# Row numbers of a three-layer decoder from one-hot products, with the order changed at attention's ends and in the second half

## The reference

```python
x = _layernorm(x + _L0_attn_ref(x, ...))     # causal attention, 16 heads of 32
x = _layernorm(x + _L0_xattn_ref(x, itok, ctx, ctx, ctx))
#   expert of a token: min(token id // 6250, 3); y = (silu(x @ W.T) * (x @ W.T)) @ W.T, W = ctx[expert]
x = _layernorm(x + _L0_ffn_ref(x, ...))
#   8 experts of width 352, the top 2 by softmax, weighted by their probabilities,
#   plus sigmoid(x @ Wsg) * shared, a gated product of width 1408
```

## Time and profile before

| | |
|---|---|
| runs, us | 1242.27, 1242.53, 1243.09 (median 1242.53) |
| the profiled execution, us | 1241.76, span 1239.0 |
| busy share of the span | TensorE 95%, VectorE 55%, ScalarE 37%, GpSimd 23% |
| TensorE's clock, mean granted | 0.979 of full |
| granted clock 32 to 36, 36 to 38, 38 to 40, 60 to 74 | 1.00, 0.60, 0.55, 0.50 to 0.57 |
| granted clock 602 to 679, 1057 to 1067, 1083 to 1117 | 1.00, 0.83, 1.00 |
| attention, second layer, third layer | 0 to 434, 435 to 571, 571 to 1239 |
| shared steps 2 to 21, experts' tiles, steps 22 to 43 | 602 to 772, 772 to 1041, 1034 to 1228 |
| loading of a ScalarE function table, us | 1.28, four times |

### The profile page before, as it was taken

How to read it: one execution, slowest core, us unless ns; L and a number is a source line. 1 busy time by engine, 2 the same in 40 slices (tenths; PEclk the granted TensorE clock), 3 DMA queues, 4 the chain that set the end, 5 groups by cost and what they waited for, 6 DMA issues and landing times.

```text
span 1239.0 us, 20363 instructions
## 1 busy us (share of the span) xinstructions
PE 1173.0 (95%) x6452; PEld 934.7 (75%) x6452; DVE 684.7 (55%) x1490; ACT 453.6 (37%) x703; POOL 279.8 (23%) x405
## 2 busy tenths in 40 slices
PE   7789999999998789998999999999999998899996
PEld 5556666676675568887777888899999997778885
DVE  5575666656656647765467434434434433676744
ACT  3245434435436223322333333344444433233331
POOL 3012314414415401223123430000000001442302
PEclk8989999999999989999999999999999999899998
DMA  7347673522533233333165673345345423555530
GB/s 249 79 117 245 197 270 102 138 68 80 144 85 112 93 119 93 114 117 119 35 96 144 235 267 105 124 138 168 132 152 158 160 76 117 167 177 164 169 120 34
DMA packets 128814, 169.76 MB, mean 137 GB/s; under 512 B 18112, under 2 KB 71360, under 8 KB 128704
## 3 DMA queue, kind: packets, MB, share of 16 engines
q1 hardware_dynamic: 110368, 128.77, 34.6%
q0 software_dynamic: 10336, 32.53, 7.3%
q10 hardware_dynamic: 8000, 7.10, 2.4%
HBM read 95.98 MB, written 47.19 MB: 116 GB/s over the span
## 4 chain that ended last, share of the span: by engine, by line
PE 73%; DVE 8%; DMA 7%; POOL 3%; ACT 2%; issue 2%; SPq 2%; ACTq 2%; POOLq 0%; DVEq 0%
PE bank L852 27%; PE bank L915 13%; PE psT L482 12%; PE psS L548 3%; DMA shared_raw<-in_L_ffn_Sd_dram 3%; PE psO L587 3%; PE bank L1547 2%; PE bank L1548 2%; PE bank L1549 2%; PE psE L569 2%; PE psN L587 2%; SPq L362 2%; PE bank L1569 1%; POOL routed_rows_io L1454 1%; DVE shared_held L1871 1%
## 5 line engine op out<-in xcount | busy, mean ns | idle before, releaser
L915 PE MATMUL bank<-store,shared_held 128*128 128x512 f32 (+1 forms) x840 | 188.4, 380 | 7.5 <-DVE shared_held L1871 7.2
L915 PEld LDWEIGHTS bank<-store,shared_held 128*128 128x128 f32 x840 | 152.5, 189 | 39.6 <-DVE shared_held L1871 9.9
L482 PE MATMUL psT<-store 128*128 128x512 f32 x576 | 157.6, 409 | 4.7 <-DVE store L701 3.0
L657 ACT ACTIVATE acc<-psE 128x512 f32<-128x512 f32 x160 | 92.7, 598 | 133.1 <-PE psE L569 88.8
L787 DVE CUSTOM_DVE_ANT_0 psS<-psS,attn_mask 128x512 f32<-128x512 f32 (+3 forms) x256 | 119.8, 512 | 35.3 <-PE psS L548 35.1
L482 PEld LDWEIGHTS psT<-store 128*128 128x128 f32 x576 | 106.2, 195 | 24.4 <-issue 3.4
L1454 POOL DMA_INDIRECT routed_rows_io<-sorted_y,routed_pos x32 | 36.8, 1149 | 380.2 <-DMA sorted_y<-routed_rows_io 313.0
L852 PE MATMUL bank<-shared_held,routed_h_hi 128*128 x624 | 115.8, 328 | 0.3 <-DVE routed_h_lo L1912 0.3
L424 POOL TENSOR_SCALAR_AFFINE_SELECT acc<-acc 128x256 f32<-128x256 f32 (+1 forms) x160 | 56.9, 362 | 258.7 <-ACT acc L657 258.3
L852 PEld LDWEIGHTS bank<-shared_held,routed_h_hi 128*128 128x128 f32 x624 | 100.3, 188 | 1.2 <-issue 0.9
L852 PE MATMUL bank<-store 128*128 x351 | 91.4, 404 | 0.0
(11 more groups left out here) (270 smaller groups left out, 2015.4 us busy)
## 6 DMA issues: line engine op xcount, KB each, us to landing
sorted_x<-attn_zero SPq DMA_DIRECT2D x19, 768.0 KB, 6.2
shared_raw<-in_L_ffn_Sg_dram SPq DMA_DIRECT2D x44, 256.0 KB, 3.1
shared_raw<-in_L_ffn_Su_dram SPq DMA_DIRECT2D x44, 256.0 KB, 3.6
shared_raw<-in_L_ffn_Sd_dram SPq DMA_DIRECT2D x44, 256.0 KB, 4.8
routed_rows_io<-sorted_x SPq DMA_DIRECT2D x39, 256.0 KB, 2.9
sorted_y<-routed_rows_io SPq DMA_DIRECT2D x39, 256.0 KB, 2.1
attn_qS<-attn_ch_hi SPq DMA_DIRECT2D x128, 64.0 KB
routed_gu_raw<-in_L_ffn_Wg_dram SPq DMA_DIRECT2D x8, 704.0 KB, 4.5
```

What stands on the lines that cost most here:

```text
L482: last = pe.matmul(out, lhs[a](k), rhs[c](k), start=(s[-1] == 0 and k == 0), stop=(s[-1] == 2 and k == KC - 1))
L657: act.activation(p_f[:, u, :], psE[:, n % 2, :], ACT.Exp, scale=SCALE).then_inc(exp_done, 1)
L915: last = pe.matmul(out, w[:, slot, at + k * P:at + (k + 1) * P], x_part(k), start=(g == 0 and k == 0), stop=(g == 2 and k == KC - 1))
```

## The change

1. **Row numbers.** `token_rows`, `number`, the sixteen scatters and the read are gone. `place` is kept as float32. After step 10 VectorE works out each token's tile and row within it (`token_tiles`), after steps 12 and 13 a one-hot matrix of the rows (`token_hot`), and ahead of step 15 TensorE adds sixteen bf16 products of 128x128 by 128x32 (`tokens`); VectorE reads them (`read_tokens`) before it goes on with step 15. TensorE's third of the six product groups of `shared_up(15)` waits for that read. SP waits for the numbers in step 16, GpSimd before the first gather.
2. **Second half.** Tile 0 is added after step 23, tiles 1 and 2 after step 24, the others after step 22 + t as before; tiles 0 to 7 are normed one step later. Of the last four tiles, ScalarE scales and shifts three (`centre` on VectorE makes the shift), and VectorE's gated adds stand one tile ahead of the statistics.
3. **Attention's start.** `wp_lo` is made by GpSimd. All twelve K transfers of group 2 are SP's, and ScalarE issues none for it.
4. **Attention's end.** The last sequence's PR, LN1, LN2 and ST follow each other tile by tile. The last four CW tiles come with one transfer after the first PV of the last group, and go through four banks that are free by then, without the shared ones.
5. The semaphores `ident_done`, `onehot_done` and `place_done` are merged with others, with the counts adapted.

```diff
@@ attention_steps
-    steps += product("PR", b, 0) + product("PR", b, 1) + [("LN1", b, 0)]
-    steps += product("PR", b, 2) + [("LN2", b, 0), ("LN1", b, 1), ("ST", b, 0)]
-    steps += product("PR", b, 3) + [("LN1", b, 2), ("LN2", b, 1), ("LN1", b, 3), ("ST", b, 1)]
-    for i in (2, 3):
-        steps += [("LN2", b, i), ("ST", b, i)]
+    steps += product("PR", b, 0) + [("LN1", b, 0)] + product("PR", b, 1) + [("LN1", b, 1), ("LN2", b, 0), ("ST", b, 0)]
+    steps += product("PR", b, 2) + [("LN1", b, 2), ("LN2", b, 1), ("ST", b, 1), ("LN2", b, 2), ("ST", b, 2)]
+    steps += product("PR", b, 3) + [("LN1", b, 3), ("LN2", b, 3), ("ST", b, 3)]
     steps += [("CW", n) for n in range(10, 16)]
@@ attention, SP
-                    for r, part in enumerate(parts[:3 - qk]):
+                    for r, part in enumerate(parts[:2] if qk == 1 and g > 2 else parts):
                         for i in range(4):
-                            if (qk, g, r) == (1, 2, 1):
-                                continue
                             sp.dma_start(dst[r * D:(r + 1) * D, i, :].bitcast(F32),
...
+                if s == ("PV", NG - 1, 0):
+                    sp.wait_ge(pv_done, QT * (NG - 1) + 1)
+                    sp.dma_start(p_f[:, 0:KC, :], ctx_w[E - 1].rearrange("(k p) n -> p k n", p=P)).then_inc(w_in[3], 16)
@@ attention, GpSimd ahead of its steps
+            pool.wait_ge(w_hi_done, 5)
+            pool.tensor_tensor(wp_lo[:], p_f[:, 0:4, :], wp_hi[:].bitcast(F32), ALU.subtract).then_inc(wp_lo_done, 1)
@@ attention, ScalarE
-                    if qk == 1 and g >= 2:
+                    if qk == 1 and g > 2:
...
@@ attention, VectorE
-                    if s == ("V", 0, 2, 2):
-                        dve.wait_ge(w_hi_done, 5)
-                        dve.tensor_tensor(wp_lo[:], p_f[:, 0:4, :], wp_hi[:].bitcast(F32), ALU.subtract).then_inc(w_lo_done, 1)
@@ routed_phase
-        FINAL_AT = {PART + t: t for t in range(HALF * QT)}
+        FINAL_AT = {PART + 1 + t: t for t in range(HALF * QT)}
...
-        ADD_AT = {PART + t: t for t in range(NT)}
+        TOKEN_AT = 15
+        ADD_AT = {PART + 1: [0], PART + 2: [1, 2]}
+        ADD_AT.update({PART + t: [t] for t in range(3, NT)})
@@ routed_phase, GpSimd
-            for t in range(NT):
-                pool.wait_ge(s_h, 1 + t // 2)
-                pool.indirect_dma_start(out=token_rows, out_offset=bass.IndirectOffsetOnAxis(ap=place[:, t:t + 1], axis=0),
-                                        in_=number[:, t:t + 1], in_offset=None).then_inc(ids_out, 16)
...
             def store_out(t):
-                pool.wait_ge(out_done, t + 1)
+                if t in LAST[:-1]:
+                    pool.wait_ge(shifted_out, t - LAST[0] + 1)
+                else:
+                    pool.wait_ge(out_done, min(t, LAST[0]) + 1)
@@ routed_phase, TensorE
+            def tokens():
+                pe.wait_ge(sel_done, 3)
+                pe.wait_ge(s_h, TOKEN_AT - 1)
+                out = s_up[TOKEN_AT % 2][:, 0:2 * NT]
+                for t in range(NT):
+                    last = pe.matmul(out, hot[:, t, :], halves[:, t].rearrange("p h j -> p (h j)"), start=(t == 0), stop=(t == NT - 1))
+                last.then_inc(count_full, 1)
@@ routed_phase, ScalarE, after its last unit
+            for i, t in enumerate(LAST[:-1]):
+                act.wait_ge(centred, i + 1)
+                act.activation(acc[:, t, :], acc[:, t, :], ACT.Identity, bias=minus_mean[:, t:t + 1], scale=rstd[:, t:t + 1]).then_inc(shifted_out, 1)
@@ routed_phase, VectorE
+            def token_tiles():
+                dve.wait_ge(consts, 7)
+                shape = [P, NT, NT]
+                then(dve.memset(upto[:, :, NT], 0.0))
+                then(dve.tensor_tensor(upto[:, :, 0:NT], bcast(place[:], shape, 2), bcast(iota128[:], shape, 1), ALU.is_ge))
+                then(dve.tensor_reduce(tiles_up, upto[:, :, 0:NT], AX, ALU.add))
+                then(dve.scalar_tensor_tensor(inner, tiles_up, -float(P), place[:], ALU.mult, ALU.add))
+                then(dve.tensor_tensor(in_tile, upto[:, :, 0:NT], upto[:, :, 1:NT + 1], ALU.subtract))
+                then(dve.tensor_scalar(halves[:, :, 0, :], in_tile, pcol, None, ALU.mult))
+                then(dve.tensor_tensor(halves[:, :, 1, :], in_tile, bcast(iota128[:], shape, 2), ALU.mult))
+
+            def token_hot(part):
+                tiles = slice(part * NT // 2, (part + 1) * NT // 2)
+                shape = [P, NT // 2, P]
+                dve.tensor_tensor(hot[:, tiles, :], bcast(inner[:, tiles], shape, 2), bcast(irow, shape, 1), ALU.is_equal).then_inc(sel_done, 1)
...
-            for i, t in enumerate(LAST):
-                shared_out(NQ - 1, [i])
+            shared_out(NQ - 1, [0])
+            dve.wait_ge(s_read, LAST[0] + 1)
+            moments(LAST[0])
+            shared_out(NQ - 1, [1])
+            make_h(HALVES + 1)
+            low_h(HALVES + 1)
+            for i, t in enumerate(LAST[1:], 1):
                 dve.wait_ge(s_read, t + 1)
                 moments(t)
-                if i == 0:
-                    make_h(HALVES + 1)
-                    low_h(HALVES + 1)
-                if i:
-                    normalise(t - 1)
+                centre(t - 1)
+                if i + 1 < QT:
+                    shared_out(NQ - 1, [i + 1])
             normalise(LAST[-1])
```

More of the change, by code:

```diff
@@ L146, in attention_phase @@
     for s in steps:
-        if s[0] in SHARED and (s[0] not in PARTS or s[-1] == 0):
+        if s[0] in SHARED and not (s[0] == "CW" and s[1] >= (E - 1) * KC) and (s[0] not in PARTS or s[-1] == 0):
             key = s[:-1] if s[0] in PARTS else s
@@ L762, in _ @@
                     then(dve.tensor_reduce(picked1, picked, AX, ALU.add))
-                    dve.tensor_copy(place[:], picked1).then_inc(place_done, 1)
-                    dve.wait_ge(place_done, 1)
+                    then(dve.tensor_copy(place[:], picked1))
                 elif kind in ("Q", "K") and s[-1] == 2:
@@ L1173, in chosen_phase, with routed_phase @@
     return [(stored[r], 16 * ((NS - r + 3) // 4)) for r in range(4)]
-def routed_phase(nc, sems, store, ident, powm, acc, x2_in, x2_of, packed, place, number, token_rows, weights, bank, chosen_y, chosen_stored, out_dram, sorted_x, sorted_y, experts, shared):
+def routed_phase(nc, sems, store, ident, powm, acc, x2_in, x2_of, packed, place, weights, bank, chosen_y, chosen_stored, out_dram, sorted_x, sorted_y, experts, shared):
     NT, C = acc.shape[1:]
@@ L1469, in _ @@
                     pool.drain()
-                if n in ADD_AT and ADD_AT[n] + 2 < NT:
-                    gather(ADD_AT[n] + 2)
+                for t in ADD_AT.get(n, []):
+                    if t + 2 < NT:
+                        gather(t + 2)
                 if n in FINAL_AT:
@@ L2057, in _ @@
                     shared_out(HALF)
-                if n in ADD_AT:
-                    routed_add(ADD_AT[n])
+                for t in ADD_AT.get(n, []):
+                    routed_add(t)
                 if n in FINAL_AT:
```

119 lines of the change are left out of this document (78 added, 41 removed).

## The result

The changed kernel takes 1227.88 us in the median of four runs (1224.78 to 1229.22), the kernel before 1242.4 beside it (1242.06 to 1243.09): a ratio of 0.9873, 95% interval 0.9851 to 0.9894. The forecast was 1225.5 with a range to 1232. The profiled execution took 1227.31 with a span of 1225.6, 13.4 less than the span before. By execution times it is 14.5 less: the profiled execution before was 2.8 us longer than its span, this one 1.7.

What follows compares the result with a forecast made beforehand. TensorE, 95% busy, bounds the kernel, so only its gaps and slow stretches are worth anything. 3.5 + 2.8 + 2.4 + 3.3 - 1.2 + 4.7 + 1.4 = 16.9 us won gives 1225.5 us, range 1219.5 to 1232 (8 in 10).

Steps and rivals of the forecast that it cites:

- Part 1: Attention's first group: wp_lo on GpSimd removes TensorE's wait (2.0 us) and the slow clock behind it (1.5): 3.5 us won.
- Rival D: Attention's first group: GpSimd's wp_lo split blocks VectorE's row maxima, 2.8 us lost there, 1231.8 us in all; chance 0.05.
- Part 2: Attention's group 2: K stacks all on SP free ScalarE's exponential, TensorE's idle goes: 2.8 us won, bounds 0 to 5.3.
- rival B: Attention's group 2: K stacks on one queue land after 73, gaining 0, 1228.3 us in all; chance 0.12.
- so the gain lasts: Attention's group 1: K reaches ScalarE's queue 3.5 us sooner, and its twelve issues are the path to 54.3.
- Part 3: Attention's end: tile-by-tile order issues the last scatter near 427.7 in place of 430.03: 2.4 us won, bounds 1.0 to 3.0.
- Part 4: Shared steps: dropping four-byte-row scatters wins 3.3 us (2.95 late steps, 0.3 first gathers); sixteen added products cost 1.2 with the switch.
- Part 5: Second half: later adds remove TensorE's 6.9 us stop and slow clock; 4.7 us won by up(32), bounds 3.0 to 8.7.
- VectorE then bounds the steps with adds and a norm: Second half, steps 23 to 30: these steps take 8.57 us against 8.19, giving back some of the gain.
- Rival A: Second half, step 24: two gather pairs stop TensorE near 3 us and the clock falls; 1228.5 us in all; chance 0.12.
- Part 6: Tail: VectorE loses two normalisations and one gated add, gains two tiny products: 1.4 us won, bounds 0.5 to 2.

Runs made afterwards that it cites:

- part 1 undone: Changed kernel with wp_lo split by VectorE after V of the third tile again, as before: 1232.66 us, ratio 0.9918 to the kernel before.
- two zero-writes: Changed kernel with two zero-writes per attention group in place of four: 1227.08 us alone; with GpSimd's fills held back and power ahead of gathers too, 1219.91 us.

## Why the prediction was right, point by point

- **Part 1** was right in size: 3.5 forecast, 3.6 in the trace. Its two terms do not stand alike. The wait, 2.0, came back when the part was undone (2.2 at group 1). The slow clock behind it, 1.5, did not: it followed waits of 1.86 and 1.83 us in the two profiles with the old attention, and not the 1.93 us of the kernel with part 1 undone. So the 3.5 holds against an execution in which the clock fell there, and I had taken that as given; how often it falls, three profiles don't tell. The two things I had left open came out as taken: GpSimd's long split, 4.61 us where I had estimated 5.1, held no row maximum up (0.70 us). Rival D falls. The rule of the Trainium skill, "SBUF — State Buffer", "Who interferes with whom", on the shared port pair agrees: the maxima have one SBUF input. The same rule is what the start shows from the other side: weight splits with two SBUF inputs beside GpSimd's fills took 5.59 us in place of 2.45. I had weighed the rule for the instruction that the change moved, and not for the overlaps that were there already and that the missing iota shifts.
- **Part 2** was mis-sized by 0.6: 3.4 against 2.8. The stacks landed in time (a wait of 0.20 us), and rival B falls. The 2.8 was TensorE's idle time alone; the low clock around it, 60 to 74 in the table before, lasted only from 60 to 67 this time, which the sum had not counted. How much of the 0.6 that is, no run separates.
- **What the sum lacked** is a term between the parts: "so the gain lasts" holds for the gap of group 1 and not, in this pair of profiles, for the groups that follow, in which 2.2 us were given back. Of that 0.7 lie between 113 and 155 us, in the stretch of SyncE's queue. Another 0.8 lie between K of group 15 and the first projection product: the clock granted from 385 to 389 was 0.57 in the changed kernel, with nearly the same waits as before, where it had been full. This is chance: four profiles had it full there and took 57.9 to 58.1 us, ten had it low and took 58.4 to 58.8. Whether the change gives anything back at all is open. From the first scores of group 2 to the first projection product it is 336.2 us in the profile before and 338.4 in the changed kernel, but 338.5 in the kernel before without its four-byte scatters, which has the old attention, and 337.6 to 338.9 in the others with four zero-writes. Only with two zero-writes is it as short as before (335.5 and 336.1).
- **Part 3** failed in size, 1.6 against 2.4. The last add came at 421.12, 11.7 us behind the first projection product where it had been 11.2, as in the new order VectorE ends the third tile's norm first. What I hadn't counted is the third scatter, which stands ahead of the last power on GpSimd: issued at 422.42 for 0.96 us, it held the power 0.5 us beyond its statistics. The forecast 3.2 us from add to scatter were 3.7.
- **Part 4** was right in its gain (2.8 of 2.95 when nothing else was changed; 0.4 for the gathers). The sixteen products cost 0.4 us in place of 1.1: the step ahead of them lasts 8.61 us where the others last 8.19. Their starts stand 0.025 us apart, and the 0.56 of the row holds the length of the last one too. I had taken 0.07 from two neighbours. Whether the scatters slowed the loads by their size or by their number, no run separates.
- **Part 5** was right in its sum, 4.4 in the trace and 4.7 when undone, and wrong in a cause. "VectorE then bounds the steps with adds and a norm" was a wait for GpSimd's power behind two gathers. The profile before had it: in rows 8 GpSimd's second gather is issued at 1105.31 for 0.95 us, the power comes behind it, and only then, at 1107.43, VectorE's split. I took the length of the step and did not ask what filled it. So the number came out right for a reason that was wrong, and would have misled in the next change: VectorE's work was not what had to be cut.
- **Rival A** is real and a matter of chance: in three of seven profiles the clock fell at the 2.85 us stop so that it cost 1.6 us, in the one taken for the changed kernel it did not. I gave it 0.12 and two prices, 1.8 in part 5's bounds and 3.0 in the rival; the lower one is near. The runs of the changed kernel spread over 4.4 us; two stops behind each of which the clock is sometimes low, at 1.6 us each, and the start's 1.4 would make that, though no run shows that they do.
- **Part 6** was right: 1.3 against 1.4. The end now hangs on GpSimd, whose last power and issues stand behind one another.

By spans the miss is 3.5 us (13.4 of 16.9): the late start (1.4), what was given back (2.2), part 3 (0.8) and small terms (0.6), less what came out better in parts 1 and 2 and between attention and the shared steps (1.4). By the medians it is 2.4. In the profiled pair the difference is the 1.1 us by which the execution before was longer outside its span. That 1.1 us is luck, and so is the full clock at both later stops of the profiled run, each worth 1.6 us where it falls.

## What to carry to other kernels

When a step is longer than the work of the engine that seems to pace it, find the wait inside it: one power moved ahead of two DMA issues on the same queue was worth more (5.8 us by the medians, 5.2 by the trace) than any part of this change. A gain in one stage lasts only while no queue behind it is full; look at the queues of the next stages before adding it up. What a dropped instruction shifts by 0.1 us can decide who gets a shared resource first. Where a kernel's wait leaves the clock in doubt, compare stretches from landmark to landmark, and look at the clock's column in each, before a median is read as the worth of an edit, and take the same stretch from every profile whose code is the same there: that is its scatter.

## What the hardware showed that I had not expected

- Two VectorE subtractions with both inputs in SBUF took 1.23 us each alone and up to 5.7 together beside GpSimd casts over four partitions; whether they did hung on which began first, the subtraction or the second cast, and they were less than 0.2 us apart.
- After one and the same wait of 2.06 us TensorE's next four products took from 1.19 to 2.08 us in different profiles of nearly the same program; after 2.85 us, 24 products took 5.74 or 8.64.
- Sixteen bf16 products of 128 x 128 by 32 columns, each with weights of its own, started 0.025 us apart.
